# Attention phase of a graph kernel: the output bias is added on VectorE instead of GpSimd, and the logits go ahead of the row transposes on TensorE

## The reference

```python
q, k, v = x @ Wq + bq, x @ Wk + bk, x @ Wv + bv        # 8 heads of 16
attn = einsum('ehd,ehd->eh', q[dst], k[src]) * scale + edge_bias
attn = softmax of attn over the edges of one target
out  = segment_sum(attn[:, :, None] * v[src], dst)     # [N, 128]
x    = layernorm(x + out @ Wo + bo)
```

## Time and profile before

| | us |
|---|---|
| median of three runs | 2579.2 (2573.97 to 2580.22) |
| the profiled execution's own time | 2575.73 |
| its span in the profile | 2573.9 |
| attention phase in the trace | about 265 to 687 |
| busy in the whole span: GpSimd / VectorE / TensorE / ScalarE | 1813.9 / 1568.6 / 1422.3 / 861.3 |
| mean granted TensorE clock, share of full | 0.767 |

### The profile page before, as it was taken

The page is one execution under the profiler, slowest core; times in us unless marked ns, Lnnn a source line. Parts: engine busy times, 40 slices in busy tenths (PEclk is TensorE's granted clock), DMA queues, the critical chain, the costliest instruction groups (busy, mean ns, idle before and its releaser), DMA issues. The chain is left out here.

```text
span 2573.9 us, 21863 instructions
## 1 busy us (share of the span) xinstructions
PE 1422.3 (55%) x4580; PEld 737.9 (29%) x4580; DVE 1568.6 (61%) x4901; ACT 861.3 (33%) x1813; POOL 1813.9 (70%) x1444
## 2 busy tenths in 40 slices
PE   6788488887456667267777367354454650011111
PEld 1344244444223333123333144222222430011110
DVE  8889277777538899857777544243344555434433
ACT  0111157776426677615665411111112330000000
POOL 5764777877188884055776778787875878877887
PEclk8899699999678888678898687777777875555555
DMA  1111344443345566244554476667797873323331
GB/s 24 26 33 36 80 119 130 124 128 84 84 96 129 138 153 157 64 109 98 123 123 112 77 198 191 151 183 177 183 170 198 224 205 94 84 63 72 75 71 43
DMA packets 358129, 297.95 MB, mean 116 GB/s; under 512 B 110941, under 2 KB 312428, under 8 KB 357981
## 3 DMA queue, kind: packets, MB, share of 16 engines
q1 hardware_dynamic: 260397, 225.43, 32.3%
q0 software_dynamic: 97600, 71.11, 14.2%
HBM read 199.75 MB, written 96.70 MB: 115 GB/s over the span
## 5 line engine op out<-in xcount | busy, mean ns | idle before, releaser
L2080 PE MATMUL tl_pX<-k_ident,tl_ga 125*128 125x125 f32 x400 | 85.4, 352 | 428.0 <-DMA tl_ga<-table_TE,k_s_idxE 326.3
L2191 DVE TENSOR_TENSOR_SCAN tl_S<-tl_same,tl_S,tl_pX 128x500 f32<-128x500 bf16 x96 | 120.3, 1253 | 317.3 <-PE tl_pX L2080 181.0
L479 POOL DMA_INDIRECT tl_ga<-table_TE,k_s_idxE x200 | 244.6, 1223 | 63.4 <-issue 59.1
L2080 PEld LDWEIGHTS tl_pX<-k_ident,tl_ga 125*128 125x128 f32 x400 | 58.1, 179 | 443.7 <-DMA tl_ga<-table_TE,k_s_idxE 336.4
L479 POOL DMA_INDIRECT eq_ga<-table_T,k_idxS x100 | 124.5, 1245 | 82.9 <-ACT eq_y L1785 53.8
L479 POOL DMA_INDIRECT at_ga<-x,k_src x100 | 139.6, 1396 | 43.4 <-issue 25.2
L479 POOL DMA_INDIRECT ms_ga<-table_T,k_idxS x100 | 135.5, 1355 | 47.0 <-issue 28.7
L1269 PE MATMUL tl_pCon<-dr_BC,dn_cT 128*128 128x512 f32 x196 | 132.9, 767 | 49.9 <-ACT dn_cT L1276 28.9
L479 POOL DMA_INDIRECT tl_ga<-table_TH,k_send x100 | 122.5, 1225 | 52.1 <-issue 51.8
L281 POOL DMA_INDIRECT table_ptab<-k_ef,ix_scatI x100 | 124.3, 1243 | 47.9 <-issue 47.9
L479 POOL DMA_INDIRECT at_gb<-xw,at_dstI x100 | 129.5, 1295 | 30.5 <-issue 30.5
(11 more groups left out here) (464 smaller groups left out, 4358.3 us busy)
## 6 DMA issues: line engine op xcount, KB each, us to landing
dr_x<-x SPq DMA_DIRECT2D x97, 256.0 KB, 5.6
result<-dr_o SPq DMA_DIRECT2D x97, 256.0 KB, 3.8
dm_xT<-xT SPq DMA_DIRECT2D x32, 768.0 KB, 6.0
tl_fac<-table_dinv SPq DMA_DIRECT2D x50, 250.0 KB, 4.9
table_T<-at_y SPq DMA_DIRECT2D x50, 224.0 KB
table_T<-ms_y SPq DMA_DIRECT2D x50, 224.0 KB
table_T<-eq_y SPq DMA_DIRECT2D x50, 224.0 KB
table_TE<-tl_y SPq DMA_DIRECT2D x50, 224.0 KB
```

The source lines that it names most:

```text
L479: nc.gpsimd.indirect_dma_start(out=buf[:, k, :], out_offset=None, in_=table, in_offset=bass.IndirectOffsetOnAxis(ap=index[:, CT * c + k:CT ...
L2080: last = nc.tensor.transpose(pX[j % 2][:, k * TP:(k + 1) * TP], ga[j % RG][:, k, :], K["ident"][0:TP, 0:TP])
L2191: nc.vector.tensor_tensor_scan(S[i][:], same[j % RM][:], pX[i][:, 0:CE], 0.0 if j % NC == 0 else S[1 - i][:, CE - 1:CE], ALU.mult, ALU.add ...
```

## The change

The add moves from GpSimd's `biased` into VectorE's `residual`, in front of its wait for the row transposes; `row_stats` gets a wait for its result. On TensorE, logits(s + 1) is called ahead of rows(s - 1). The waits of `fetch` are unchanged.

```diff
@@ GpSimd
-            def biased(c):
-                have_a(pool, c)
-                need(pool, s_y, c - 2)
-                nc.gpsimd.tensor_tensor(z[c % 3][:, CT:2 * CT, :], ga[c % RA][:], bc(bo, CT), ALU.add).then_inc(s_z2, 1)
-
             for s in range(-3, NC):
                 if live(s + 3):
                     fetch(s + 3)
-                if live(s):
-                    biased(s)
@@ TensorE
                 if live(s + 2):
                     turn_targets(s + 2)
+                if live(s + 1):
+                    logits(s + 1)
                 if live(s - 1):
                     rows(s - 1)
-                if live(s + 1):
-                    logits(s + 1)
@@ VectorE
             def residual(c):
-                dve.wait_ge(s_z2, c + 1)
+                have_a(dve, c)
                 have_b(dve, c)
+                need(dve, s_y, c - 2)
+                nc.vector.tensor_tensor(z[c % 3][:, CT:2 * CT, :], ga[c % RA][:], bc(bo, CT), ALU.add).then_inc(s_z2, 1)
                 dve.wait_ge(s_psR, c + 1)
                 nc.vector.tensor_copy(K["pay"][:, CT * c:CT * c + CT, 3], gb[c % RB][:, :, D])
                 nc.vector.tensor_tensor(z[c % 3][:, 0:CT, :], gb[c % RB][:, :, 0:D], pR[0:TP, :].rearrange("p (k f) -> p k f", k=CT), ALU.add).then_inc(s_z, 1)
                 dve.wait_ge(s_z, c + 1)
+                dve.wait_ge(s_z2, c + 1)
                 row_stats(nc, z[c % 3], 2 * CT, st[c % 2], mv, s_d)
```

## The result

The changed kernel takes 2796.25 us (median of four, 2793.01 to 2797.45), the one before 2576.88 beside it: a ratio of 1.0849 (95% interval 1.083 to 1.0868), 8.5% slower. The forecast was 2814 us in a range of 2762 to 2846, slower with a chance of 0.95. The profiled execution took 2797.45 us, its span is 2795.7, 221.8 us more than before.

A forecast was written before the change was run, and what follows sets the result against it. TensorE and GpSimd were read as both near full in the attention phase. Twenty rounds of 26.4 us from turn_targets(4) at 344.6 put turn_targets(24) 232.8 us later; with +2, together +235: 2814 us, range 2762 to 2846.

The forecast's parts named there:

- the ring: Attention phase: add of chunk k releases gathers of k+4, which lead through TensorE to the add of k+1; 26.4 us.
- round: Once around from one chunk's add to the next chunk's: 26.4 us, where a step took 15.4.
- landing: From the end of the last gather's issue to the target transposes: 2.3 us.
- add: The output bias add on VectorE: 0.7 us per chunk.
- release of GpSimd: From VectorE's add to GpSimd's first gather: taken 0.3 us, its ordinary gap; up to 0.91.
- eight gathers: GpSimd's gathers of one chunk, with part of VectorE's work beside them: 12.8 us.
- turn to add: From the target transposes to the end of wide, where residual starts with the add: 10.3 us.
- the tail: Behind turn_targets(24): no gather waited for; four adds less some logits waits make +2 us.
- The warm clock: Rival, chance 0.15: TensorE's clock stays up, so 24.3 us per chunk and 2772 us in all.
- Faster, since GpSimd was the bound: Rival, chance 0.03: GpSimd's step falls to 13.5 us, TensorE's to 14.8; 12 us gained, 2567 us.
- VectorE grows by 17 us: Rival, chance 0.03: unseen slack, so only 25 adds of 0.68 us come on top; 2596 us.
- The wait that is one chunk looser: Rival, chance 0.02: fetch's wait doesn't bind the engines; gain and cost meet near 2579 us.

The follow-up runs named there:

- e3: The changed kernel with five ga buffers instead of four: 2556.16 us, ratio 0.9925.
- e4: The changed kernel, four ga buffers, with the add still on VectorE but at the head of step s: 2551.45 us, ratio 0.9911.
- e2: The changed kernel with TensorE's old order (row transposes ahead of logits): 2795.28 us, ratio 1.0855.
- e5: The changed kernel with gb gathered ahead of ga in fetch, so only the ga gathers stand behind the wait for the add: 2583.53 us, ratio 1.003.
- e7: The changed kernel with extra matmuls, results overwritten, in TensorE's gap, only in the 21 steps whose next turn waits: 2757.09 us, ratio 1.0717.
- e8: The kernel before with the add on VectorE at the head of step s, TensorE's old order kept: 2570.07 us, ratio 0.9988.
- e1: The kernel before with only TensorE's order changed (logits ahead of row transposes), add on GpSimd: 2565.04 us, ratio 0.9969.
- e10: The kernel before with logits ahead of row transposes and five ga buffers, add on GpSimd: 2563.75 us, ratio 0.9967.

## Why the prediction was right, and where its sizes were off

**The mechanism** was the forecast one. The wait count of `fetch` was unchanged, but who raises it and when had moved 12 us behind the moment at which it was needed. e3 and e4 open the ring in two different ways and all 220 us go; e2 shows that the order on TensorE has no part in it; e5 takes four gathers (6.0 us) and the part from the target to the source transposes (4.9 us) out of it, and the round falls by 9.9 us, since the landing grew by 1.1.

**The terms.** Forecast against the mean of 21 rounds:

| | forecast | measured |
|---|---|---|
| add | 0.7 | 0.68 |
| release of GpSimd | 0.3 | 0.91 |
| eight gathers | 12.8 | 12.12 |
| landing | 2.3 | 2.33 |
| turn to add | 10.3 | 9.72 |
| round | 26.4 | 25.76 |

Release was the term that was off most for its size: it was taken at GpSimd's ordinary gap, while the nearest row, 0.91 us behind its own add, was only the upper end. It is 0.91 us here too (0.90 to 0.92 in all 21), behind an instruction of another engine. So the pause in rows 2 belongs to this wait and not to GpSimd's own add. Gathers and turn were too large by 0.7 and 0.6 us. For the turn I leaned on chunk 24, whose burst was at the low clock for 5 us; here most rounds alternate between about 9.1 and 10.1 us, as the granted clock comes back 2.8 to 3.3 us or 4.7 to 5.6 us into the burst. Twenty rounds too long by 0.67 us (25.73 between the turns) are 13 us; the tail took 47.7 us as before (47.6), not 2 more; turn_targets(4) came at 345.36, not 344.6. That is the 14 us between 2811 forecast for the profiled execution and 2797.45. The medians, 2814 forecast and 2796.25, lie 18 us apart; most of the other 4 us is that the forecast was put against a median of 2579.2 for the kernel before, which was 2576.88 beside the changed kernel.

**The rivals.** The warm clock did not come by itself: the granted clock was 0.50 at the head of a burst. Its price was put at 2.1 us a round; e7 gave back 1.7 in the mean, 1.9 in the 18 rounds without the low clock. The Trainium skill (TensorE: Matmul & The Clock Gate, section "HAM oscillation — how this bites in real kernels") says that a loop with DMA waits between bursts pays the low clock each time; the runs agree, and add that this was the smaller part: the wait itself cost some 180 us, the clock 35 to 40.

"Faster, since GpSimd was the bound" falls twice: the ring closed, and where it is open (e8) relieving GpSimd alone gives 0.1%. Here the reading ahead of the forecast was too weak. I took a GpSimd that never waits for an engine as full, in balance with TensorE. But its 15.38 us step was partly drawn out by VectorE (below), and once TensorE's step shrank (e1), GpSimd's shrank with it to 14.9 in the mean, its eight gathers from 13.1 to 12.7. It is full at 14.9 (12.7 + 0.91 + 1.28), and it is then the bound of the mean step: the target transposes waited for gb 12.0 us instead of 8.2, and with the add gone from it and a fifth buffer (e3) the mean step is 14.5. So in the kernel before it stood just under the bound, which is why both halves are needed for the 24 us of e4. "VectorE grows by 17 us" falls with e4. The wait that is one chunk looser falls with GpSimd's 21 waits of 13.7 us.

**What the profile showed as forecast:** GpSimd waits 287.5 us (280), TensorE 9.3 us a turn (9), adds 26 us apart in steps with and without moments, a mean clock of 0.77 in the phase, hardly a wait for oF. The phase ended at 907.7 us, not near 922, by the same 14 us.

## What to carry to other kernels

When an operation moves to another engine, follow every semaphore that it raises: a wait whose text is unchanged may now be answered a step later. Write the circle out, from the release through the DMA and the consumer back to the release; divide its length by the number of chunks that it lets past in one round, and if that is longer than the step, it sets the time, whatever the busy shares say. Here 25.8 us for one chunk stood against a step of 15.4, and with the fifth buffer 12.9. One more buffer or an earlier place in the same engine's step opens it; here either turned 8.5% slower into 0.8 to 0.9% faster.

## What the runs showed of the hardware

**Gathers and VectorE.** How long a gather holds GpSimd depends on what VectorE is doing when the gather starts. I sorted the gathers of the phase by VectorE's instruction 0.1 us after their start. In the kernel before, the 17 that began within the scan L817 (three inputs, all in SBUF) took 2.10 us in the mean, 19 that began within the subtraction L802 (both inputs in SBUF) 1.58; 79 beside an idle VectorE took 1.21, none more than 1.23, and so did 12 beside the scan L800, one of whose inputs is in PSUM. The order decides, as two places of e5 show (timelines of VectorE and GpSimd):

```profile
496.40 1.24 DVE L810 TENSOR_TENSOR_SCAN at_Nu<-at_f,at_Nu,at_pv 128x500 f32<-128x500 f32 x1
496.67 1.98 POOL L479 DMA_INDIRECT at_gb<-xw,at_dstI  x1 [0.30 <-issue]
...
510.27 1.29 POOL L479 DMA_INDIRECT at_gb<-xw,at_dstI  x1 [0.30 <-issue]
510.46 1.23 DVE L810 TENSOR_TENSOR_SCAN at_Nu<-at_f,at_Nu,at_pv 128x500 f32<-128x500 f32 x1
```

The first gather starts 0.27 us into the scan and takes 1.98 us; the second starts 0.19 us ahead of it and takes 1.29. The Trainium skill (GPSIMD Engine Reference, section "8. Key points") names contention between GpSimd and VectorE instructions with two SBUF inputs; the rows agree, for the first part of an indirect DMA at least. That it is the reading of the indices there which is held up is a guess that no run tested. In e4, 6 gathers that began within the moved add took 1.62 us.

**Release of a gather.** For the first ga gather of a chunk 0.91 us pass between the end of the bias add that it waits for and its start, whether the add was on GpSimd or on VectorE; gathers that wait for nothing follow at 0.30. It is not the price of every released gather. The first gb gather that waited for VectorE's residual add (L837 in e4 and e8, L840 in e10) started 0.29 to 0.30 us behind its end, in all 42 such waits of e4, e8 and e10 (one of e8, timelines of VectorE and GpSimd):

```profile
392.36 0.68 DVE L837 TENSOR_TENSOR at_z<-at_gb,at_pR 125x512 f32<-125x512 f32 x1
393.34 1.21 POOL L479 DMA_INDIRECT at_gb<-xw,at_dstI  x1 [2.86 <-DVE at_z L837]
```

In `fetch` two `need` calls stand ahead of the ga gathers and one ahead of the gb gathers; whether that makes the difference no run tested.

**Landing.** From the last issue's end to the transposes it took 2.1 to 2.9 us in the changed kernel, where SyncE's load starts some 7 us ahead of that end (618.06 against 625.06 in the round above), and up to 5.4 us in e5, where the load can fall into the landing.
